# bf16 copies stored over six steps, the second step's tokens loaded later, half of the high angle tables built by GpSimd, the first statistics moved behind the recurrence

## The chip, the cores and the metric

The kernel runs on all eight cores of one Trainium2 chip. Each core takes one of the eight sequences, computes it alone and exchanges nothing with the others. The time is that of the slowest core, in microseconds of the device. Five engines have instruction streams of their own: PE (TensorE, matrix products), DVE (VectorE), ACT (ScalarE), POOL (GpSimd) and SP (SyncE, which here only issues transfers). Transfers run on 16 DMA engines per core, fed by a queue of SP and a queue of POOL.

## The reference

One sequence has 8192 tokens of 1024 numbers. What is computed, cut to the core:

```python
xn = layernorm(x)                                   # over the 1024 features
# recurrence, complex, one state per p (1024 of them)
Lambda = exp(-exp(nu_log) + 1j*exp(theta_log))
Bu = einsum('ph,blh->blp', (B_re + 1j*B_im)*exp(gamma_log)[:, None], xn)
xs[t] = Lambda * xs[t-1] + Bu[t]
s  = real(einsum('hp,blp->blh', C_re + 1j*C_im, xs)) + D*xn
# feed-forward, 1024 -> 4096 -> 1024
g  = silu(relu(xn @ W1 + b1) @ W2 + b2)
out = x + s*g
```

The inputs and weights are float32; the kernel multiplies in bfloat16 and adds up in float32.

## The kernel before

The 8192 tokens go through in 16 steps of 512 (`NSTEP`). In every step all weights pass through SBUF once: they are laid out as 24 chunks (`NCH`) of 128 x 4096 numbers, in the order c0 to c23 of the list `ORDER`: B0, W1_0, B1, W1_1, B2, W1_2, B3, W1_3, W1_4 to W1_7, W2_0 to W2_3, C_0 and C_1, W2_4 to W2_7, C_2 and C_3. A chunk of B, W1 or W2 is used by 32 matmuls of 512 columns. The two C chunks of a half are used together, by 64 matmuls (`cx`), and no earlier than both have landed. The chunks share five slots (`RING = 5`, n % 5, where n = 24 k + c counts chunks over the steps): chunk n may be loaded when the matmuls of chunk n-5 are done (`consumed`).

A chunk gets into its slot in one of two ways. A **cast** (line 257) reads 2 MB of float32 from HBM and writes 1 MB of bfloat16 into the slot; POOL issues it. A **load** (line 215) reads the 1 MB of bfloat16 that the kernel has stored in its HBM tensor `wb`; SP issues it. The **store** of that copy (`keep`, line 200) is issued by SP from the slot, once the cast has landed; until it has landed the slot can't be refilled. `KEEP_STEP[c]` is the step in which chunk c is stored: up to that step it is cast, after it loaded. SP's queue also carries the tokens x of the next step (2 MB, line 231; for step 1 line 221) and the results, two halves of 1 MB per step (lines 224, 227). SP goes through n = 0, 1, 2, ... in order: at place n come the load of n if it is one, the store of chunk n-4 if it is due, then tokens and results. Whatever it waits for holds back all that stands behind it. POOL goes through the casts in order in the same way.

In a step, PE computes Bu for state groups m = 0 to 7 (128 states each, two per B chunk, line 322) between the first W1 chunks (line 333), then W2's first half (line 345), C's first half (line 360), W2's second half with the transposes of the next step's tokens between (line 288), and C's second half. ACT copies Bu out of PSUM into one of four buffers `vv` (line 433, buffer m % 4, which needs DVE's first two products on group m-4 to be done, `v_u`) and the W1 results into `h1` (line 439). Its order is fixed: vv0, vv1, four of h, vv2, vv3, four of h, ..., so that a late `vv` holds back the h behind it, and with them PSUM banks 4 to 7, which PE's W1 groups take in turn. For group m, DVE turns Bu back by the angle of each token with tables of cosines and sines (`cS`, `sS`, 512 columns for each of the eight groups), runs the real recurrence (line 636) and turns the result forward again (`state`, lines 626 to 654). C needs all eight groups (`v_xs`).

The tables are built in step 0 by DVE, by doubling: level lv fills columns 2^lv to 2^(lv+1) from the ones below with six instructions (`double`, lines 574 to 581). Levels 0 to 5 are done for all groups at once (`tables_low`), levels 6 to 8 for groups 0 to 3 before group 0 and for groups 4 to 7 before group 4 (`tables_high`). The statistics of the next step's layer norm (`ln_stats`, lines 506 to 513) come before group 7.

Of the kernel before, what the change touches and what calls it, by code (L numbers as in the profile page):

```python
# [10 lines left out]
ALU = mybir.AluOpType  # L11
# [4 lines left out]
N = 512  # L16
NSTEP = T // N
CH = H // 128
# [16 lines left out]
PLACE = {c: i for i, c in enumerate(ORDER)}  # L35
RING = 5

KEEP_STEP = [(0, 2, 1, 2)[c % 4] for c in range(NCH)]


def is_cast(n):
# [16 lines left out]
def build_program():  # L58
# [15 lines left out]
    def sem(name):  # L74
        return es.enter_context(nc.semaphore(name))
# [66 lines left out]
    v_out = sem("v_out")  # L142

    p_id = sem("p_id")

    nu, th, gam, b1 = par[:, 0:8], par[:, 8:16], par[:, 16:24], par[:, 24:56]
    r_tab = ab[:, 0:8]
# [44 lines left out]
    def sync_program(eng):  # L192
# [17 lines left out]
        for n in range(NCH * NSTEP):  # L210
            k, c = n // NCH, n % NCH
            if not is_cast(n):
                slot_free(n)
                eng.wait_ge(*kept(first_kept(n)))
                eng.dma_start(ring[n % RING][:, :],
                              bass.AP(wb_d.ap().tensor, c * 128 * 4096,
                                      [[4096, 128], [1, 4096]])).then_inc(d_w[n % RING], 16)
            if n >= RING - 1 and is_kept(n - RING + 1):
                keep(n - RING + 1)
            if n == 8:  # L220
                eng.dma_start(xt[1][:, :], x_rows(1)).then_inc(d_x[1], 16)
            if c == NCH - 1:
                eng.wait_ge(v_out, 8 * k + 4)
                eng.dma_start(out_rows(k, 0), xt_half(k, 0)).then_inc(d_out[0], 16)
            if c == 5 and k >= 1:
                eng.wait_ge(v_out, 8 * k)
                eng.dma_start(out_rows(k - 1, 1), xt_half(k - 1, 1)).then_inc(d_out[1], 16)
            if c == 8 and 1 <= k < NSTEP - 1:
                for h in range(2):
                    eng.wait_ge(d_out[h], 16 * k)  # L230
                eng.dma_start(xt[(k + 1) % 2][:, :], x_rows(k + 1)
                              ).then_inc(d_x[(k + 1) % 2], 16)
# [11 lines left out]
    def gpsimd_program(eng):  # L244
        eng.memset(dx[:, 0:128], 1.0).then_inc(p_id, 1)
        eng.wait_ge(p_id, 1)
        eng.affine_select(dx[:, 128:256], dx[:, 0:128], [[1, 128]], ALU.is_equal, 0.0,
                          base=0, channel_multiplier=-1).then_inc(p_id, 1)
        eng.wait_ge(d_x0[1], 16)
        for n in range(3 * NCH):  # L250
            if not is_cast(n):
                continue
            if n >= RING:
                eng.wait_ge(*consumed(n - RING))
                if is_kept(n - RING):
# [2 lines left out]
                          bass.AP(w_d.ap().tensor, (n % NCH) * 128 * 4096,  # L258
                                  [[4096, 128], [1, 4096]])
                          ).then_inc(d_cast[n % RING], 16)  # L260
            if n == 6:
                for dst, src in ((d_rep, dv_d), (b2_rep, b2_d)):
                    eng.dma_start(dst[:, :], bass.AP(src.ap().tensor, 0, [[0, 128], [1, H]])
                                  ).then_inc(d_rows, 16)
# [222 lines left out]
    def vector_program(eng):  # L487
# [93 lines left out]
            t = mark(eng.tensor_tensor(seg(sS, n), seg(sS, n), tb_, ALU.add))  # L581
            eng.wait_ge(*t)

        def tables_low():

            mark(eng.memset(view(cS, 0, [[CH * N, 128], [N, CH]]), 1.0))
            t = mark(eng.memset(view(sS, 0, [[CH * N, 128], [N, CH]]), 0.0))
# [13 lines left out]
            eng.wait_ge(*t)  # L601
            for lv in range(6):
                double(lv, 0, CH)
            mark(eng.tensor_copy(c512, lad[:, 144:152]))
            mark(eng.tensor_scalar(view(ab, 32, [[64, 128], [2, 8]]), lad[:, 152:160], -1.0, None,
                                   ALU.mult))
            mark(eng.tensor_copy(view(ab, 33, [[64, 128], [2, 8]]), lad[:, 152:160]))

        def tables_high(first):
            for lv in range(6, 9):  # L610
                double(lv, first, 4)

        P1, P2 = pq[:, 0:2 * N], pq[:, 2 * N:4 * N]

# [78 lines left out]
        first_finish(2)  # L693
        angles()
        first_finish(3)
        tables_low()
        for k in range(NSTEP):
            turn[0] += CI
            for m in range(CH):
                if k == 0 and m % 4 == 0:  # L700
                    tables_high(m)
                if m == CH - 1 and k + 1 < NSTEP:
                    ln_stats(k + 1)
                state(k, m)
            if k + 1 < NSTEP:
                ln_finish(k + 1)
            if k == 0:
# [55 lines left out]
```

## Time and profile before

| | us |
|---|---|
| median of 3 runs (lowest, highest) | 2754.15 (2751.19, 3036.26) |
| profiled execution, its own time | 2755.06 |
| span of its slowest core, core 4 | 2753.9 |
| span of its fastest core, core 1 | 2727.4 |
| PE busy, share of the span | 2683.8, 97% |
| DVE busy | 1906.7, 69% |
| POOL busy | 30.6, 1% |

The span runs from the first to the last instruction of a core; the device's own time of the profiled execution is 1.2 us more. Busy time of PE counts overlapping matmuls whole, so the starts in its timeline say more than its sum. All rows below are of core 4 where nothing else is said. A row of the timeline stands for a run of like instructions; what stands in brackets is the idle time before it and what ended that.

### The profile page before, as it was taken

How to read it: one execution, taken by the hardware profiler on the slowest of the kernel's cores; microseconds unless marked ns; L12 is line 12 of the kernel's file. 1: busy time of each engine (PE TensorE's matmuls, PEld its weight loads, DVE VectorE, ACT ScalarE, POOL GpSimd, SP SyncE). 2: the span in 40 equal slices, each digit the busy share in tenths (PEclk: the TensorE clock that was granted, in tenths of full speed). 3: DMA queues.
4: the chain of work that ended last, by engine and by line, in shares of the span. 5: the costliest groups of instructions: out<-in, count | busy, mean ns of one | idle time of the engine just before them, and what ended most of it. 6: DMA issues, size and time to landing. Idle time of an engine off the chain costs nothing.

```text
span 2753.9 us, 35106 instructions; the slowest of 8 cores (2727.4 to 2753.9 us)
## 1 busy us (share of the span) xinstructions
PE 2683.8 (97%) x12545; PEld 1235.0 (45%) x12800; DVE 1906.7 (69%) x2684; ACT 765.5 (28%) x1018; POOL 30.6 (1%) x62
## 2 busy tenths in 40 slices
PE   6889998999999999999999999999999999999999
PEld 3344443444444444444444444444444444444444
DVE  7949659287593965849577594875939759395674
ACT  4222323223232322313223132231322323132220
POOL 1000000000000000000000000000000000000000
PEclk9999999999999999999999999999999999999998
DMA  9999988874544545445454454545545355464542
GB/s 189 190 186 211 211 199 226 237 256 143 184 183 168 199 145 187 182 146 213 163 204 154 160 201 161 198 153 182 185 164 197 136 191 184 153 214 151 180 153 99
DMA packets 84793, 498.28 MB, mean 181 GB/s; under 512 B 7568, under 2 KB 7568, under 8 KB 32400
## 3 DMA queue, kind: packets, MB, share of 16 engines
q1 hardware_dynamic: 76560, 438.36, 45.1%
q0 software_dynamic: 8064, 57.68, 13.0%
q8 instruction: 105, 1.72, 0.3%
q14 instruction: 64, 0.52, 0.1%
HBM read 493.91 MB, written 58.72 MB: 201 GB/s over the span
## 4 chain that ended last, share of the span: by engine, by line
PE 89%; DMA 10%; issue 1%; DVE 1%; SPq 0%; DVEq 0%; POOLq 0%
PE PS L345 31%; PE PS L333 27%; PE PS L360 16%; PE PS L322 13%; DMA wb<-ring 4%; DMA ring<-w 4%; PE PS L288 1%; DMA out<-xt 1%; DMA ring<-wb 0%; DMA xt<-x 0%; PE PS L301 0%; DVE dx L679 0%; DVE xt L682 0%; DVE dx L676 0%; DVE dx L672 0%
## 5 line engine op out<-in xcount | busy, mean ns | idle before, releaser
L333 PE MATMUL PS<-xT,ring 128*128 128x512 bf16 x4001 | 893.5, 381 | 29.6 <-DMA ring<-w 16.3
L345 PE MATMUL PS<-ring,h 128*128 128x512 bf16 x4017 | 892.1, 380 | 4.2
L333 PEld LDWEIGHTS PS<-xT,ring 128*128 128x128 bf16 x4096 | 402.1, 98 | 513.2 <-issue 34.4
L345 PEld LDWEIGHTS PS<-ring,h 128*128 128x128 bf16 x4096 | 398.7, 98 | 470.7 <-issue 6.9
L659 DVE TENSOR_TENSOR gg<-PS,b_rep 128x512 f32<-128x512 f32 x128 | 88.3, 692 | 613.6 <-PE PS L345 613.6
L439 ACT ACTIVATE h<-PS,par_s 128x512 bf16<-128x512 f32 x512 | 352.5, 689 | 519.5 <-PE PS L333 518.4
L322 PE MATMUL PS<-xT,ring 128*128 128x512 bf16 x1999 | 447.3, 379 | 2.0 <-DMA ring<-w 0.2
L636 DVE TENSOR_TENSOR_SCAN yy<-ab,carry,pq 128x512 f32<-128x512 f32 x256 | 314.2, 1269 | 0.0
L322 PEld LDWEIGHTS PS<-xT,ring 128*128 128x128 bf16 x2032 | 198.7, 98 | 240.2 <-issue 0.7
L433 ACT ACTIVATE vv<-PS,ab 128x1024 bf16<-128x1024 f32 x128 | 142.8, 1116 | 537.5 <-PE PS L322 513.5
L360 PE MATMUL PS<-ring,xsr 128*128 128x512 bf16 x1006 | 243.8, 382 | 7.8 <-DMA ring<-w 6.7
L360 PE MATMUL PS<-ring,xsi 128*128 128x512 bf16 x994 | 242.8, 382 | 1.6
L427 ACT ACTIVATE xT<-PS 128x512 bf16<-128x512 f32 x128 | 69.7, 596 | 472.8 <-PE PS L288 472.7
L627 DVE TENSOR_TENSOR pq<-vv,cS 128x1024 f32<-128x1024 bf16 x128 | 156.8, 1225 | 28.6 <-DVE xsi L652 16.6
L360 PEld LDWEIGHTS PS<-ring,xsr 128*128 128x128 bf16 x1024 | 100.7, 98 | 129.9 <-issue 13.8
L643 DVE TENSOR_TENSOR pq<-yy,cS 128x1024 f32<-128x1024 f32 x128 | 156.1, 1219 | 0.2 <-issue 0.2
L647 DVE TENSOR_TENSOR pq<-yy,sS 128x1024 f32<-128x1024 f32 x128 | 156.2, 1220 | 0.0
L360 PEld LDWEIGHTS PS<-ring,xsi 128*128 128x128 bf16 x1024 | 100.8, 98 | 123.0 <-issue 6.8
L628 DVE TENSOR_TENSOR pq<-vv,sS 128x1024 f32<-128x1024 bf16 x128 | 155.9, 1218 | 0.0
L676 DVE TENSOR_TENSOR dx<-dx,PS 128x512 f32<-128x512 f32 x128 | 88.1, 689 | 72.3 <-PE PS L360 55.9
L446 ACT ACTIVATE gg<-gg 128x512 f32<-128x512 f32 x128 | 78.9, 629 | 170.9 <-DVE gg L659 170.7
L679 DVE TENSOR_TENSOR dx<-dx,gg 128x512 f32<-128x512 f32 x128 | 88.6, 693 | 23.2 <-DVE dx L676 23.2
(72 smaller groups left out, 1023.8 us busy)
## 6 DMA issues: line engine op xcount, KB each, us to landing
ring<-wb SPq DMA_DIRECT2D x330, 1024.0 KB, 4.9
ring<-w POOLq DMA_DIRECT2D x54, 1024.0 KB, 17.6
out<-xt SPq DMA_DIRECT2D x31, 1024.0 KB, 8.8
xt<-x SPq DMA_DIRECT2D x15, 2048.0 KB, 10.1
wb<-ring SPq DMA_DIRECT2D x24, 1024.0 KB, 14.5
xt<-x SPq DMA_DIRECT2D x4, 512.0 KB, 7.2
out<-xt SPq DMA_DIRECT2D x4, 256.0 KB, 2.0
d_rep<-Dv POOLq DMA_DIRECT2D x1, 512.0 KB, 30.4
```

The source lines that it names most:

```text
L322: inst = eng.matmul(bk(2 * (m % 2) + comp), w[:, o:o + 128], xT[:, kc * N:(kc + 1) * N], start=(kc == 0), stop=(kc == CH - 1))
L333: inst = eng.matmul(bk(b), w[:, o:o + 128], xT[:, kc * N:(kc + 1) * N], start=(kc == 0), stop=(kc == CH - 1))
L345: inst = eng.matmul(bk(tb), h1[:, o:o + 128], w[:, kl * 512:(kl + 1) * 512], start=(q == 0 and kl == 0), stop=(q == 3 and kl == 7), skip_g ...
L360: inst = eng.matmul(bk(b), xs[:, o:o + 128], w[comp][:, pc * 512:(pc + 1) * 512], start=(comp == 0 and pc == 0), stop=(comp == 1 and pc == ...
L433: eng.activation(vv[m % 4][:, :], bk(2 * (m % 2), 2), AF.Identity, scale=gam_t[:, m:m + 1]).then_inc(a_vv, 1)
L439: eng.activation(h1[:, mi * N:(mi + 1) * N], bk(b), AF.Relu, bias=b1[:, mi:mi + 1]).then_inc(a_h1, 1)
L627: mark(eng.tensor_tensor(p1, u3, cc, ALU.mult))
L628: t = mark(eng.tensor_tensor(p2, us, ss, ALU.mult), v_u)
L636: y = mark(eng.tensor_tensor_scan(yy[:, j * N:(j + 1) * N], rb, wb, carry[:, 2 * m + j:2 * m + j + 1], ALU.mult, ALU.add))
L643: q = mark(eng.tensor_tensor(p1, y3, cc, ALU.mult))
L647: q = mark(eng.tensor_tensor(p2, ys, ss, ALU.mult))
L679: t = mark(eng.tensor_tensor(dx[:, :], dx[:, :], gg[:, tb * 512:(tb + 1) * 512], ALU.mult))
```

## The change

Four edits. (1) `KEEP_STEP` becomes a list by chunk with values 0 to 5, where it was 0, 2, 1, 2 in turn: 2 chunks are stored in step 0, 1 in step 1, 2 in step 2, 4 in step 3, 9 in step 4 and 6 in step 5. A chunk is cast until it is stored, so there are 107 casts, where there were 54, and POOL's loop goes over six steps. (2) The tokens of step 1 are requested when chunk 8 has been used, not before. (3) Levels 6 to 8 of the tables of groups 4 to 7 are built by POOL, in six parts of three instructions, one part behind each of the casts n = 6 to 11; DVE waits for them before group 4. DVE builds the other half where it did. The copies of D and b2 to all partitions are issued behind cast 14, not 6. (4) The statistics of step 1 come behind group 7, not before it, and so do not stand between groups 6 and 7 in step 0; in the other steps they stay.

```diff
-KEEP_STEP = [(0, 2, 1, 2)[c % 4] for c in range(NCH)]
+KEEP_STEP = [4, 5, 4, 3, 4, 5, 4, 4, 2, 5, 4, 3, 1, 4, 5, 0, 3, 4, 5, 2, 4, 0, 3, 5]
+LAST_KEEP = max(KEEP_STEP)
...
             if n == 8:
+                eng.wait_ge(*consumed(n))
                 eng.dma_start(xt[1][:, :], x_rows(1)).then_inc(d_x[1], 16)
...
+        def high_part(j):
+
+            lv, half = 6 + j // 2, j % 2
+            n = 1 << lv
+
+            def seg(tab, at):
+                return bass.AP(tab, 4 * N + at, [[CH * N, 128], [N, 4], [1, n]])
+
+            def each(off):
+                return bass.AP(lad, lv * 16 + off + 4, [[160, 128], [1, 4], [0, n]])
+
+            tmp = bass.AP(gg, half * 4 * 256, [[TB * 512, 128], [n, 4], [1, n]])
+            if j == 0:
+                eng.wait_ge(v_tab, 4)
+            elif half == 0:
+                eng.wait_ge(p_tab, 3 * j)
+            if half == 0:
+                eng.tensor_tensor(tmp, seg(sS, 0), each(8), ALU.mult).then_inc(p_tab, 1)
+                eng.tensor_tensor(seg(cS, n), seg(cS, 0), each(0), ALU.mult).then_inc(p_tab, 1)
+                eng.wait_ge(p_tab, 3 * j + 2)
+                eng.tensor_tensor(seg(cS, n), seg(cS, n), tmp, ALU.subtract).then_inc(p_tab, 1)
...
         eng.wait_ge(d_x0[1], 16)
-        for n in range(3 * NCH):
+        for n in range((LAST_KEEP + 1) * NCH):
             if not is_cast(n):
                 continue
...
-            if n == 6:
+            if 6 <= n <= 11:
+                high_part(n - 6)
+            if n == 14:
                 for dst, src in ((d_rep, dv_d), (b2_rep, b2_d)):
...
-        def tables_low():
+        def tables():
...
-            mark(eng.tensor_copy(c512, lad[:, 144:152]))
+            mark(eng.tensor_copy(c512, lad[:, 144:152]), v_tab)
...
-        def tables_high(first):
             for lv in range(6, 9):
-                double(lv, first, 4)
+                double(lv, 0, 4)
...
             for m in range(CH):
-                if k == 0 and m % 4 == 0:
-                    tables_high(m)
-                if m == CH - 1 and k + 1 < NSTEP:
+                if k == 0 and m == 4:
+                    eng.wait_ge(p_tab, 18)
+                if m == CH - 1 and 1 <= k < NSTEP - 1:
                     ln_stats(k + 1)
                 state(k, m)
+            if k == 0:
+                ln_stats(1)
```

POOL's order in step 0, from its first cast on, before (`ring` is a slot, `w` the float32 weights):

```order
L257 DMA ring<-w 128x4096 x7
L263 DMA d_rep<-Dv 128x1024
L263 DMA b_rep<-b 128x1024
L257 DMA ring<-w 128x4096 x47
```

and in the changed kernel, from the fourth part on (`gg` holds the temporary product, `lad` the factors of each level):

```order
L288 DMA ring<-w 128x4096
L275 TENSOR_TENSOR gg<-cS,lad 128x512
L276 TENSOR_TENSOR sS<-sS,lad 128x4x128
L278 TENSOR_TENSOR sS<-sS,gg 128x4x128
L288 DMA ring<-w 128x4096
L270 TENSOR_TENSOR gg<-sS,lad 128x1024
L271 TENSOR_TENSOR cS<-cS,lad 128x4x256
L273 TENSOR_TENSOR cS<-cS,gg 128x4x256
L288 DMA ring<-w 128x4096
L275 TENSOR_TENSOR gg<-cS,lad 128x1024
L276 TENSOR_TENSOR sS<-sS,lad 128x4x256
L278 TENSOR_TENSOR sS<-sS,gg 128x4x256
L288 DMA ring<-w 128x4096 x3
```

Three products or sums on 256, 512 or 1024 numbers per partition now stand between two casts on POOL's stream.

SP's order over steps 0 and 1 before, from the tokens of step 0 on:

```order
L205 DMA xt<-x 128x1024 x3
L200 DMA wb<-ring 128x4096 x2
L221 DMA xt<-x 128x4x1024
L200 DMA wb<-ring 128x4096 x3
L224 DMA out<-xt 128x4x512
L215 DMA ring<-wb 128x4096
L200 DMA wb<-ring 128x4096
```

and in the changed kernel:

```order
L207 DMA xt<-x 128x1024 x3
L224 DMA xt<-x 128x4x1024
L202 DMA wb<-ring 128x4096
L227 DMA out<-xt 128x4x512
L202 DMA wb<-ring 128x4096
L230 DMA out<-xt 128x4x512
L234 DMA xt<-x 128x4x1024
L217 DMA ring<-wb 128x4096
```

Of the six stores of step 0 two are left, and none stands before the tokens of step 1.

## Rows read from the trace of the kernel before

**Rows 1.** The page: busy time, share and instructions of PE.
```profile
PE 2683.8 (97%) x12545; PEld 1235.0 (45%) x12800; DVE 1906.7 (69%) x2684; ACT 765.5 (28%) x1018; POOL 30.6 (1%) x62
```

**Rows 2.** Span and granted clock of two cores.
```profile
core 1: 2727.4 us, clock 0.996
...
core 4: 2753.9 us, clock 0.991
```

**Rows 3.** Timeline of PE: start, length, instructions, [idle before <-what ended it].
```profile
83.97 37.24 PE L333 MATMUL PS<-xT,ring 128*128 128x512 bf16 x157 [11.05 <-DMA ring<-w]
...
155.58 2.29 PE L360 MATMUL PS<-ring,xsr 128*128 128x512 bf16 x5 [6.74 <-DMA ring<-w]
...
215.20 7.07 PE L322 MATMUL PS<-xT,ring 128*128 128x512 bf16 x31
...
266.48 29.26 PE L333 MATMUL PS<-xT,ring 128*128 128x512 bf16 x125 [2.77 <-DMA ring<-w]
298.26 7.07 PE L333 MATMUL PS<-xT,ring 128*128 128x512 bf16 x31 [2.52 <-DMA ring<-w]
...
389.83 7.07 PE L322 MATMUL PS<-xT,ring 128*128 128x512 bf16 x31
...
467.20 1.87 PE L333 MATMUL PS<-xT,ring 128*128 128x512 bf16 x4 [8.14 <-DMA ring<-wb]
...
567.76 7.07 PE L322 MATMUL PS<-xT,ring 128*128 128x512 bf16 x31
581.58 7.07 PE L322 MATMUL PS<-xT,ring 128*128 128x512 bf16 x31
...
735.31 7.07 PE L322 MATMUL PS<-xT,ring 128*128 128x512 bf16 x31
```

**Rows 4.** DMA queues from 85 to 155 us: packets, MB, share of 16 engines.
```profile
q0 software_dynamic: 1410, 10.24, 93.0%
q1 hardware_dynamic: 339, 2.43, 8.6%
```

**Rows 5.** The same queue and stretch on core 1.
```profile
q0 software_dynamic: 1437, 10.46, 90.4%
```

**Rows 6.** The page: SP's queue over the whole span.
```profile
q1 hardware_dynamic: 76560, 438.36, 45.1%
```

**Rows 7.** Chain of waits from 215 to 300 us: start, length, what.
```profile
248.87 36.63 DMA wb<-ring
...
286.02 12.00 DMA ring<-w
```

**Rows 8.** Timeline of DVE in step 0.
```profile
48.98 1.23 DVE L627 TENSOR_TENSOR pq<-vv,cS 128x1024 f32<-128x1024 bf16 x1 [0.17 <-DVE sS L581]
...
81.24 1.22 DVE L628 TENSOR_TENSOR pq<-vv,sS 128x1024 f32<-128x1024 bf16 x1
...
90.39 0.43 DVE L574 TENSOR_TENSOR pq<-sS,lad 128x256 f32<-128x256 f32 x1
...
103.48 1.23 DVE L627 TENSOR_TENSOR pq<-vv,cS 128x1024 f32<-128x1024 bf16 x1 [0.17 <-DVE sS L581]
...
134.60 4.85 DVE L506 BATCH_NORM_STATS2 st<-xt 128x6 f32<-128x512 f32 x8 [0.17 <-DVE xsi L652]
...
140.19 1.23 DVE L627 TENSOR_TENSOR pq<-vv,cS 128x1024 f32<-128x1024 bf16 x1
...
149.70 0.69 DVE L652 SCALAR_TENSOR_TENSOR xsi<-pq 128x512 bf16<-128x512 f32 x1
```

**Rows 9.** Busy time (instructions) of PE, PEld, DVE, ACT, POOL; clock, DMA share, GB/s.
```profile
35.00:90.00 55.00, 43.51 (x187) 18.97 (x190) 52.62 (x71) 14.30 (x18) 4.78 (x9) 0.88 0.98 197
```

**Rows 10.** Timeline of ACT in step 0.
```profile
82.55 1.11 ACT L433 ACTIVATE vv<-PS,ab 128x1024 bf16<-128x1024 f32 x1 [9.25 <-DVE pq L628]
87.64 0.69 ACT L439 ACTIVATE h<-PS,par_s 128x512 bf16<-128x512 f32 x1 [3.98 <-PE PS L333]
```

**Rows 11.** Timeline of POOL in step 0.
```profile
1.40 0.29 POOL L247 TENSOR_SCALAR_AFFINE_SELECT dx<-dx 128x128 f32<-128x128 f32 x1
...
38.54 0.53 POOL L257 DMA_DIRECT2D ring<-w  x1 [2.61 <-PE PS L333]
...
73.47 0.53 POOL L257 DMA_DIRECT2D ring<-w  x1 [6.77 <-PE PS L322]
```

More of the change, by code:

```diff
@@ L144, in build_program @@
     p_id = sem("p_id")
+    p_tab = sem("p_tab")
     nu, th, gam, b1 = par[:, 0:8], par[:, 8:16], par[:, 16:24], par[:, 24:56]
@@ L248, in gpsimd_program @@
                           base=0, channel_multiplier=-1).then_inc(p_id, 1)
+        def high_part(j):
[15 more added lines that the diff above has]
+                eng.tensor_tensor(seg(cS, n), seg(cS, n), tmp, ALU.subtract).then_inc(p_tab, 1)
+            else:
+                eng.tensor_tensor(tmp, seg(cS, 0), each(8), ALU.mult).then_inc(p_tab, 1)
+                eng.tensor_tensor(seg(sS, n), seg(sS, 0), each(0), ALU.mult).then_inc(p_tab, 1)
+                eng.wait_ge(p_tab, 3 * j + 2)
+                eng.tensor_tensor(seg(sS, n), seg(sS, n), tmp, ALU.add).then_inc(p_tab, 1)
         eng.wait_ge(d_x0[1], 16)
-        for n in range(3 * NCH):
+        for n in range((LAST_KEEP + 1) * NCH):
             if not is_cast(n):
@@ L695, in vector_program @@
         first_finish(3)
-        tables_low()
+        tables()
         for k in range(NSTEP):
```

## The prediction, made before the changed kernel ran

> **What bounds the kernel now.** I read the page first: PE is busy for 97% of the span [rows 1]. The timeline of PE tells what that hides. From step 3 on a step takes 735.31 - 567.76 = 167.55 us without an idle gap, and a chunk 6.91 us, half of the distance between the two B rows at 567.76 and 581.58 [rows 3]. 24 chunks make 165.8; the other 1.75 are the transposes. So 13 of 16 steps are at PE's own pace, and no edit touches them. Time can only come or go before 568 us. Core 4 loses it at five places [rows 3]: 11.05 us idle before W1_3, 6.74 before C in step 0; 2.77 and 2.52 in step 1, which takes 389.83 - 215.20 = 174.63, that is 7.1 over; 8.14 in step 2, which takes 177.93, 10.4 over. The overs are more than the idle because PE comes back at half clock: from 83.97 to C, less the idle, lie 64.87 us for nine chunks that need 62.2, so a long gap costs 2.7 more. Every one of these gaps ends with a transfer into the ring.
>
> The DMA queues say why. Between 85 and 155 us both queues together fill more than the whole of the 16 engines [rows 4]. A cast costs 0.93 x 70 us / (10.24 MB / 1.049) = **6.67 us** of all 16; 1 MB on SP's queue costs 0.451 x 2753.9 / (438.36 / 1.049) = **2.97 us** [rows 2, 4, 6]. A step's transfers, counted so (each has 4 MB of tokens and results): step 1 has 18 casts, 6 loads, 6 stores: 167.6 us; step 2 has 12, 12, 12: 163.2. Both are just under PE's 167.55 and still lost 7.1 and 10.4. The chain of waits shows how: a store issued right behind the tokens' load took 36.63 us, POOL could refill its slot only then, and 12 us later PE got its chunk [rows 7].
>
> **The change, part by part.**
>
> *Stores over six steps.* Step 0 loses four stores and gains nothing: 24 casts and 8 MB, 183.9 us. Steps 1 to 4 become (casts, loads, stores) 22, 2, 1: 167.5; 21, 3, 2: 166.8; 19, 5, 4: 165.3; 15, 9, 9: 165.4. Step 5 (6, 18, 6) has 123.2 and is free. So two steps at 97 to 100% become four. Bounds for what such a step loses: 0, since none is over 167.55, and 10.4, the worst seen. Less store traffic speaks for the low end, and in steps 1 to 3 no store stands directly behind the tokens' load; in step 4 those of c6 and c7 do. Against it: five slots are a lead of at most four chunks, the tokens and one half of the results (9 us) fall together in each step's first half, where eight chunks of PE (55.3) meet eight casts (53.4) in steps 1 to 3, and each pair of C chunks wants the second 6.9 us early. I take the nearer row, 7.1, for each of the four: **28.4 us**, in place of 17.5.
>
> A page bears on the price: the Trainium skill, HBM Reference, § on the domain's bandwidth, says that the two cores of a pair share about 716 GB/s, some 358 each when both stream. By it a cast's 2.1 MB would be an estimated 5.9 us, and step 1 would need about 150 and lose nothing. The row, taken with all eight cores casting, has 6.67, and decides.
>
> *Later tokens.* The 2 MB (5.9 us) leave the stretch before W1_3, and so do two stores (5.9) and the D and b2 copies (3.0), while that chunk was 11.05 late. W1_3 then starts on time, near 72.9. What is late next is ACT: its vv for group 7 waited for DVE's second product on group 3 (81.24 + 1.22) and ended at 83.66 [rows 8, 10]; the first h behind it ends near 84.4 and frees the bank for W1_4. So W1_4 starts at 84.4 + L, where L is what DVE is late by then. Tokens asked for when W1_4 is done, near 111, land by 150 even if they take as long as that store did; wanted behind group 7.
>
> *High tables on POOL.* DVE loses 103.48 - 90.39 = 13.1 us between groups 3 and 4 [rows 8]; it is in nobody's way, because W1_4 depends on groups 0 to 3, and C on all eight. POOL gets 18 instructions with 3 x 2 x (256 + 512 + 1024) = 10,752 numbers per partition. The trace has no POOL product of two tensors. Low: DVE's rate, 1.22 us per 1024: 12.8 us. High: POOL's one row of arithmetic, 0.29 us for 128: 24.4 us [rows 8, 11]. The parts run between 38.5 and some 85 us, behind casts whose times PE sets [rows 11]; with at most 7 us for the longest they delay the next cast by about one cast's issue, and end before DVE wants them. What matters is L: whether POOL's reads of the same SBUF tables hold DVE, which is busy 52.62 of 55 us there [rows 9], so that nothing held is given back. Bounds for L: 0 (independent), 24.4 (each holds the other). Casts issued by POOL do not stretch a group of DVE, 10.4 us each, but they read no table. I take L = **20**, near the upper end: both engines work on two SBUF operands at once, and POOL's own row is the nearer price.
>
> The Trainium skill, SBUF — State Buffer, § on the shared port pair, speaks against this edit: DVE with two SBUF inputs and a GpSimd instruction that reads SBUF exclude each other for a whole instruction. Nothing in this trace tests it; by it L is all of POOL's time, without it the first rival below holds.
>
> With L = 20, W1_4 starts at 104.4; eight chunks and the half clock (55.3 + 2.7) give C at **162.4**. Group 7 ends at 150.4 - 13.1 - 5.6 + 20 = 151.7, not in the way, and the second C chunk, which landed by 155.3, has four stores less ahead of it and one more: 146.4. From C to the end of the step are eight chunks and the transposes, 57.0: 219.4, against 215.20: **+4.2**.
>
> *Statistics behind group 7.* Saves 140.19 - 134.60 = 5.6 us before C [rows 8]; C is 10 us later than group 7 already, so nothing. They end near 157, before W2's results.
>
> Sum against the profiled execution: 2755.06 + 4.2 + 28.4 - 17.5 = **2770 us**. Its time is 1 us above the median of the runs.
>
> **Rivals.** *POOL costs DVE nothing* (L = 0). For it: POOL's casts leave DVE's groups alone. Against: no row has both on tables. C then starts at 146.4, when its chunk lands, the step ends near 206 with half clock, -9.2: 2755.1 - 9.2 + 10.9 = **2757**.
>
> *The four steps lose nothing* (the queue's few stores are worth more than its casts). For: core 1, with 0.904 x 70 / (10.46 / 1.049) = 6.35 us per cast, has the shortest span [rows 2, 5]. Against: the slowest core counts, at 6.67. With L = 20 **2742**, with L = 0 **2728**, the only case that is plainly faster.
>
> *Casts get dearer when six steps stream them*: slower than before by over 2%. Place: steps 1 to 4 on every core, all of them over PE's pace. Each 0.1 us per cast is 7.7 us over their 77 casts. At 7.3 us they need 181.4, 180.0, 177.3 and 174.8, in all 43.3 over, which gives 2813; 7.25 is the point from which it decides. Against it: step 0 had this traffic, on eight cores, at 6.67.
>
> **How the numbers follow.** Chances: the forecast (L from 12 to 24, a loss of 5 to 10 per step) 0.46; L near 0 with the losses 0.24; L with no losses 0.14; neither 0.10; dearer casts 0.04; the rest spread, 0.02. The likeliest case gives 2770. Upper bound of its terms: L = 24.4 (+8.6) and 10.4 per step (+41.6 - 17.5): 2788. The range takes in 2742 and 2757 and leaves out 2728 and 2813: **2738 to 2788**. Nearly all cases lie within 2%, which is about what a measurement of this kernel can tell from no change: faster by over 2% (below 2700) 0.01, within 0.95, slower 0.04.
>
> **What the profile after would show.** W1_3 on time near 73 and a gap before W1_4, ended through ACT by DVE, 5 us long if L = 0 and 25 if L = 20. DVE's products of 1024 numbers longer than 1.22 us, or gaps between them, while POOL has a part: L in its sum. POOL's 18 instructions, 13 to 24 us in all. C in step 0 at 146 or 162. PE's gaps in steps 1 to 4, ended by casts, 28 in sum with the clock; step 4 with one before W1_7 or W2_0 behind the stores of c6 and c7. Steps from 5 on at 167.55. I am wrong if a gap grows in step 5 or later, if W1_3 is still late, or if casts leave 6.3 to 6.7 us.

## The result

| | us |
|---|---|
| before, beside it (median of its runs) | 2754.15 |
| after (median; lowest and highest of 5 runs) | 2766.18 (2765.5, 2766.25) |
| ratio after / before, with its 95% interval | 1.0053 [1.0035, 1.0071] |
| profiled execution, its own time | 2766.18 |
| span of its slowest core, core 3 | 2765.1 |
| span of its fastest core, core 7 | 2751.5 |

The change costs 0.5%, some 12 to 15 us; the interval allows 10 to 20. Executions in which some cores show a lower granted clock are left out of every range of times below, and of the ratios where the difference is marked, and rows come from cores and stretches that show none of it. All rows are of the slowest such core where nothing else is said. The line numbers have moved: B is line 355, W1 366, W2 378, C 393 of the changed kernel; ACT's vv 466 and h 472; DVE's first two products of a group 659 and 660.

The page has this in place of [rows 1]:

```profile
PE 2694.4 (97%) x12800; PEld 1233.6 (45%) x12800; DVE 1914.6 (69%) x2666; ACT 763.3 (28%) x1018; POOL 87.1 (3%) x133
```

PE's share is the same 97%, and again that row hides everything that happened. POOL has gone from 30.6 to 87.1 us. What answers to [rows 3] is the timeline of PE:

```profile
77.08 5.68 PE L355 MATMUL PS<-xT,ring 128*128 128x512 bf16 x16 [8.64 <-ACT vv L466]
82.60 7.07 PE L366 MATMUL PS<-xT,ring 128*128 128x512 bf16 x32
104.34 29.88 PE L366 MATMUL PS<-xT,ring 128*128 128x512 bf16 x128 [14.68 <-ACT h L472]
163.77 1.89 PE L393 MATMUL PS<-ring,xsr 128*128 128x512 bf16 x8 [1.92 <-DMA ring<-w]
220.81 7.07 PE L355 MATMUL PS<-xT,ring 128*128 128x512 bf16 x32
...
393.76 7.07 PE L355 MATMUL PS<-xT,ring 128*128 128x512 bf16 x32
...
561.58 7.07 PE L355 MATMUL PS<-xT,ring 128*128 128x512 bf16 x32
...
622.27 30.32 PE L366 MATMUL PS<-xT,ring 128*128 128x512 bf16 x128 [5.28 <-DMA ring<-wb]
737.09 7.07 PE L355 MATMUL PS<-xT,ring 128*128 128x512 bf16 x32
...
818.08 8.75 PE L366 MATMUL PS<-xT,ring 128*128 128x512 bf16 x32 [3.62 <-DMA ring<-wb]
831.24 29.47 PE L378 MATMUL PS<-ring,h 128*128 128x512 bf16 x128 [4.41 <-DMA ring<-wb]
917.59 7.07 PE L355 MATMUL PS<-xT,ring 128*128 128x512 bf16 x32
```

The starts of B0 (220.81, 393.76, 561.58, 737.09, 917.59) give the steps 172.95, 167.82, 175.51 and 180.50: 5.4, 0.3, 8.0 and 12.95 over PE's pace of 167.55, together **26.6**. The next step is at that pace and stays there.

Step 0 changed the name of its wait. The gap before W1_4 ends with ACT, and behind ACT stands DVE, which is late because of this (POOL first, then DVE in the same stretch):

```profile
66.14 1.91 POOL L270 TENSOR_TENSOR gg<-sS,lad 128x1024 f32<-128x1024 f32 x1
68.00 1.89 POOL L271 TENSOR_TENSOR cS<-cS,lad 128x1024 f32<-128x1024 f32 x1
70.03 2.61 POOL L273 TENSOR_TENSOR cS<-cS,gg 128x1024 f32<-128x1024 f32 x1
```
```profile
65.96 4.49 DVE L683 TENSOR_TENSOR xsr<-pq 128x512 bf16<-128x512 f32 x1
70.37 2.82 DVE L684 SCALAR_TENSOR_TENSOR xsi<-pq 128x512 bf16<-128x512 f32 x1
...
82.27 0.69 DVE L683 TENSOR_TENSOR xsr<-pq 128x512 bf16<-128x512 f32 x1
```

Read the two together; `xsr` and `xsi` are the two results of a group that C reads. POOL's products at 66.14 and 68.00 end at 69.89. DVE's instruction for `xsr`, which takes 0.69 us when POOL is quiet (82.27), is recorded from 65.96 and ends at 70.45: it ends 0.56 us, most of its own length, after POOL's pair. The next one ends at 73.19, 0.55 us after POOL's third at 72.64. So in these rows the two engines do not share, they take turns, and the waiting is inside DVE's recorded length: busy time hides it. Between 66 and 93 us no DVE row names POOL as what it waited for.

### The profile page after: what moved, and what is told of

Read it like the earlier page. It is cut to its first block, busy times and chain, and to the rows that moved or that the text cites. A ratio compares the mean times of both kernels' runs of the same rounds, so it can differ in the third digit from the quotient of the medians.

```text
span 2765.1 us, 35310 instructions; the slowest of 8 cores (2751.5 to 2765.1 us)
## 1 busy us (share of the span) xinstructions
PE 2694.4 (97%) x12800; PEld 1233.6 (45%) x12800; DVE 1914.6 (69%) x2666; ACT 763.3 (28%) x1018; POOL 87.1 (3%) x133
## 4 chain that ended last, share of the span: by engine, by line
PE 85%; DMA 10%; DVE 3%; issue 1%; ACT 0%; DVEq 0%; SPq 0%; POOL 0%; POOLq 0%; ACTq 0%
PE PS L378 30%; PE PS L366 27%; PE PS L393 15%; PE PS L355 13%; DMA wb<-ring 5%; DMA ring<-w 4%; PE PS L321 1%; DMA ring<-wb 1%; DVE pq L659 0%; DVE pq L660 0%; DMA xt<-x 0%; DVE yy L668 0%; DVE xsr L683 0%; DVE pq L608 0%; DVE xsi L684 0%
## 5 line engine op out<-in xcount | busy, mean ns | idle before, releaser
L366 PE MATMUL PS<-xT,ring 128*128 128x512 bf16 x4096 | 901.8, 381 | 26.1 <-ACT h L472 14.7
## 6 DMA issues: line engine op xcount, KB each, us to landing
xt<-x SPq DMA_DIRECT2D x15, 2048.0 KB, 11.3
```

What stands on the lines that cost most here:

```text
L366: inst = eng.matmul(bk(b), w[:, o:o + 128], xT[:, kc * N:(kc + 1) * N], start=(kc == 0), stop=(kc == CH - 1))
```

## The experiments

All are compared with the kernel before, run beside them. "Over" is always a step's length less 167.55. The theory of the prediction was that POOL's reading instructions hold DVE in step 0 (L = 20), and that the casts take most of what the transfers of steps 1 to 4 have to spare. The rivals to be told apart were a step 0 without L and steps without losses. The eight cores run the same program and still differ by up to 17 us in what they lose, so a row of one core is not enough; a table behind the runs has all of them.

**1. The high tables by DVE again**, everything else as changed:

```diff
-            if 6 <= n <= 11:
-                high_part(n - 6)
...
-                    eng.wait_ge(p_tab, 18)
+                    for lv in range(6, 9):
+                        double(lv, 4, 4)
```

> The changed kernel, except that DVE again builds levels 6 to 8 of groups 4 to 7, before group 4; POOL computes nothing in step 0. Theory (POOL's products hold DVE, L = 20 us, and this alone makes W1_4 late): DVE's instructions between 38 and 92 us are back at 1.22 and 0.69 us, the gap before W1_4 shrinks to about 5 us, C of step 0 starts at about 146 in place of 164, and the time is 2766 - 13 = 2753 us, give or take 4. Rival (DVE is late because casts, not products, hold it): the gap before W1_4 stays above 13 us and the time near 2766. Second rival (the lead that PE's long gap gave the queue is worth as much as the gap): steps 1 to 4 lose over 35 us in place of 27, and the time stays at 2762 or more.

Measured: 2752.9 to 2760, median 2757.1, ratio 1.0006 [0.9994, 1.0019]: as expected, at the upper edge. PE on the slowest core, 7, of an execution that took 2759.95:

```profile
83.55 29.74 PE L364 MATMUL PS<-xT,ring 128*128 128x512 bf16 x128 [5.11 <-ACT h L470]
...
207.49 7.07 PE L353 MATMUL PS<-xT,ring 128*128 128x512 bf16 x32
```

W1_4 starts 20.8 us earlier (83.55 against 104.34) and step 0 ends 13.3 us earlier. But the next four steps start at 207.49, 378.90, 547.60, 726.08 and 911.28: 3.9, 1.1, 10.9 and 17.65 over, 33.6 in place of 26.6. On the slowest core of this execution half of what step 0 gives is taken again. That is not the rule: the ratios, 1.0053 and 1.0006, differ by 13 us, which is all that step 0 gives, and over all cores the four steps lose 4 us more on average. This is the rival "POOL costs DVE nothing" made real, and at its price of 2757.

**2. The high tables on POOL alone**, put into the kernel before (edit 3 with its wait, no other):

```diff
+            if 6 <= n <= 11:
+                high_part(n - 6)
...
+                if k == 0 and m == 4:
+                    eng.wait_ge(p_tab, 18)
```

> The kernel before with edit 3 alone: POOL builds the high tables of groups 4 to 7 behind casts 6 to 11; the store list, the tokens and the statistics are as before. Theory: L = 20 again, whatever the list is: W1_4 starts near 104 in place of 93.6, C of step 0 near 162, step 0 ends 4 us later than before; with a fuller ring behind the long gap steps 1 and 2 lose a little less than their 17.5 us: 2755 to 2760. Rival (the loss needs the changed list's casts): 2754 with W1_4 at 94.

Measured: 2754.2 to 2758.4, ratio 1.0004 [0.9992, 1.0016]. The copies of D and b2 stay behind cast 6 here. On core 1:

```profile
104.81 30.29 PE L365 MATMUL PS<-xT,ring 128*128 128x512 bf16 x128 [13.09 <-ACT h L471]
...
219.60 7.07 PE L354 MATMUL PS<-xT,ring 128*128 128x512 bf16 x32
```

The same start of W1_4 (104.8) and end of step 0 (219.6) as in the full change, so L is edit 3's and no other's. It costs 4.4 us against [rows 3] there, 3.9 on the average of all cores, and the interval of the whole time has no change in it. Steps 1 and 2 lose 10.0 and 10.1, where a little less than 17.5 in sum was expected.

**3. The stores over six steps alone**, in the kernel before:

```diff
-KEEP_STEP = [(0, 2, 1, 2)[c % 4] for c in range(NCH)]
+KEEP_STEP = [4, 5, 4, 3, 4, 5, 4, 4, 2, 5, 4, 3, 1, 4, 5, 0, 3, 4, 5, 2, 4, 0, 3, 5]
```

> The kernel before with edit 1 alone, the new list of stores. Theory: step 0 gains, since no store stands before W1_3: that chunk is on time or nearly, W1_4 waits about 4 us for DVE's group 3, C of step 0 waits for DVE's group 7 at 150.4 in place of its chunk at 155.3, and step 0 ends about 5 us earlier than before; steps 1 to 4 lose 27 us as in the changed kernel, in place of 17.5 in steps 1 and 2: 2754 - 5 + 9 = 2758, give or take 5. Rival (spreading the stores is worth what it was made for): 2740 or less.

Measured: ratio 1.0023 [1.0012, 1.0034], runs of 2758.6 to 2764: at the upper edge of what was expected. Core 5:

```profile
149.36 3.57 PE L361 MATMUL PS<-ring,xsr 128*128 128x512 bf16 x8 [11.03 <-DVE xsi L653]
```

Step 0 ends at 209.02; its C waits for DVE, not for a chunk. The steps after lose 6.3, 0, 10.2 and 17.25: 33.8, as in run 1. The stores alone win 6 us in step 0 and lose 16 behind it. The losses are there without edits 2, 3 and 4.

**4. Later tokens and the moved statistics alone** (edits 2 and 4), in the kernel before:

```diff
             if n == 8:
+                eng.wait_ge(*consumed(n))
...
-                if m == CH - 1 and k + 1 < NSTEP:
+                if m == CH - 1 and 1 <= k < NSTEP - 1:
...
+            if k == 0:
+                ln_stats(1)
```

> The kernel before with edits 2 and 4 alone: the tokens of step 1 are requested when chunk 8 is used, the statistics of step 1 come behind group 7. Theory (both only move work within step 0): W1_3 is late by about 5 us in place of 11, but the tokens then stand before C's chunks, which land at about 155 as before; DVE is done with group 7 at 145 and waits for nobody: 2754, give or take 3, with up to 3 us lost again before the transposes, because the statistics hold back the combination of the results. Rival (each edit gives what it takes off its place, 6 and 5.6 us): 2743.

Measured: 2750.5 to 2753.6, ratio 1.0007 [0.9995, 1.002], as expected. Core 1:

```profile
76.23 36.06 PE L334 MATMUL PS<-xT,ring 128*128 128x512 bf16 x160 [3.05 <-DMA ring<-w]
128.56 23.38 PE L346 MATMUL PS<-ring,h 128*128 128x512 bf16 x96 [9.36 <-DMA ring<-w]
```

The wait before W1_3 falls to 3.05 us and one of 9.36 appears before W2_1, where the tokens now are. Step 0 ends at 215.16, against 215.20 in [rows 3]; over all cores it ends at 206.4 to 217.0, before at 208.8 to 217.2. The traffic was moved, not removed.

**5 and 6. What on POOL holds DVE?** Two kernels like run 1 (DVE builds all tables), in which POOL also carries 18 instructions that nobody uses, at the same six places, on a buffer of its own that DVE never touches. In the first they are products of two SBUF operands, in the second they only write, over twice as many numbers. This idle work, with one more write of that buffer at the start and DVE's wait for the work before group 4, is all that is added.

```diff
+            for i in range(3):
+                eng.tensor_tensor(t, t, t, ALU.mult).then_inc(p_tab, 1)
```
```diff
+            for i in range(3):
+                eng.memset(t, 1.0).then_inc(p_tab, 1)
```

> As tables_dve (DVE builds all tables; 2757 us), but POOL computes beside it what nobody uses: behind casts 6 to 11 three products each on private data in gg, with 256, 512 and 1024 numbers per partition as in the changed kernel. Theory (POOL and DVE exclude each other as engines, whatever the addresses): DVE's instructions stretch as in the changed kernel, W1_4 starts near 104 again in place of 83.5, C of step 0 near 163 to 165 (group 7 is 13 us later than in the changed kernel), and the time is 2768 to 2775. Rival (they clash because both read the same tables cS and sS and the factors in lad): DVE stays at 1.22 us, W1_4 at 84, 2757 us.

> As dummy_products, but POOL's instructions only write: 18 memsets of 512, 1024 and 2048 numbers per partition, which read nothing. Theory (it is POOL's reading beside DVE's two operands that holds DVE): DVE stays at 1.22 us, W1_4 at 84, and the time is tables_dve's 2757, give or take 4. Rival (any POOL instruction on SBUF holds DVE for as long as it runs): DVE is late by most of POOL's busy time, W1_4 after 92, 2765 or more.

Measured: products 2769 to 2770, ratio 1.0065 [1.005, 1.008]; writes 2751.8 to 2756.4, ratio 0.9995 [0.9977, 1.0013]. PE, POOL and DVE of core 1 with the products:

```profile
102.40 29.57 PE L351 MATMUL PS<-xT,ring 128*128 128x512 bf16 x128 [14.68 <-ACT h L457]
```
```profile
66.26 7.05 POOL L263 TENSOR_TENSOR gg<-gg 128x1024 f32<-128x1024 f32 x3
```
```profile
66.24 2.48 DVE L669 SCALAR_TENSOR_TENSOR xsi<-pq 128x512 bf16<-128x512 f32 x1
68.89 2.66 DVE L644 TENSOR_TENSOR pq<-vv,cS 128x1024 f32<-128x1024 bf16 x1 [0.17 <-DVE xsi L669]
```

And with the writes, core 1 again, PE, POOL and DVE:

```profile
83.08 7.29 PE L350 MATMUL PS<-xT,ring 128*128 128x512 bf16 x23 [5.31 <-ACT h L456]
```
```profile
65.02 5.67 POOL L262 MEMSET gg<- 128x2048 f32 x3
```
```profile
67.56 0.69 DVE L668 SCALAR_TENSOR_TENSOR xsi<-pq 128x512 bf16<-128x512 f32 x1
68.42 1.23 DVE L643 TENSOR_TENSOR pq<-vv,cS 128x1024 f32<-128x1024 bf16 x1 [0.17 <-DVE xsi L668]
```

The windows from 38 to 93 us on core 1 say the same in one row each (us, then busy time and count of PE, PEld, DVE, ACT, POOL; clock, DMA share, GB/s). Run 1, run 5, run 6:

```profile
38.00:93.00 55.00, 50.22 (x224) 22.16 (x222) 52.75 (x68) 17.02 (x22) 3.52 (x7) 0.94 1.02 167
```
```profile
38.00:93.00 55.00, 42.54 (x190) 18.58 (x188) 53.65 (x42) 10.88 (x14) 32.61 (x25) 0.93 0.92 156
```
```profile
38.00:93.00 55.00, 49.69 (x221) 21.89 (x219) 52.68 (x68) 16.80 (x22) 22.52 (x24) 0.94 0.97 163
```

DVE is almost equally busy in all three, 52.7 to 53.7 us, but gets through 68 instructions, 42 and 68. That count is where a stretched engine shows; its busy time does not. W1_4 is as late with products on a private buffer as with the tables, so it is not the shared tables that couple the engines. POOL's writes, 22 us of busy time, hold nobody. They also stand between two casts on POOL's stream for almost as long as the products (5.67 us in the row above, 7.05 with the products), so it is not later casts that make DVE late. A POOL instruction that reads one operand only was not tried.

**7. The stores of c6 and c7 in step 5, not 4**, on run 1:

```diff
-KEEP_STEP = [4, 5, 4, 3, 4, 5, 4, 4, 2, 5, ...]
+KEEP_STEP = [4, 5, 4, 3, 4, 5, 5, 5, 2, 5, ...]
```

> As tables_dve, with c6 and c7 stored in step 5 in place of step 4; two more casts. Theory (step 4 loses its 16 to 18 us because these two stores stand behind the tokens in SP's queue and their slots are wanted first by c11 and c12): step 4 loses under 7 us, step 5 gains no gap over 2 us, the gap of 6 to 8 us before c8 in step 3 stays (it is c3's store behind the results), and the time is 2757 - 11 = 2746, give or take 4. Rival (the number of bytes decides): step 4 loses as much and step 5 some more, 2757 or above.

Measured: ratio 1.0024 [1.0003, 1.0045], 2752 to 2756. A miss by 6 to 10 us, and by the ratio no faster than run 1. Core 0's steps from 1 on lose 2.7, 0.6, 6.8, **3.1** and **8.5**; over all eight cores step 4 loses 2.8 to 7.0, where run 1 loses 13.3 to 17.7, and step 5 loses 6.8 to 10.7. Step 4 gave what was expected; step 5, which loses nothing in the kernels above, now has this:

```profile
994.25 16.53 PE L376 MATMUL PS<-ring,h 128*128 128x512 bf16 x63 [5.79 <-DMA ring<-w]
```

Its chain of waits goes back through four stores in a row, three of which are shown. The first of them was issued 0.48 us behind the tokens' load, and SP had held both back until the results had landed:

```profile
895.86 31.77 DMA out<-xt
...
927.71 0.38 SPq L234
...
928.19 17.29 DMA wb<-ring
...
946.01 8.44 DMA wb<-ring
...
965.32 12.52 DMA wb<-ring
978.36 15.64 DMA ring<-w
```

So the two stores are what step 4 could not bear, and a step 5 with 8 stores can't either, though its transfers, 8 casts, 16 loads, 8 stores and 4 MB, sum to 136.5 us at the prediction's prices. The sum over a step is not the test.

**8. Another list**, on run 1: the stores are 2, 1, 2, 4, 6 and 9 from step 0 to 5, and are so placed that few follow each other; 110 casts in place of 107.

```diff
-KEEP_STEP = [4, 5, 4, 3, 4, 5, 4, 4, 2, 5, 4, 3, 1, 4, 5, 0, 3, 4, 5, 2, 4, 0, 3, 5]
+KEEP_STEP = [4, 5, 3, 4, 0, 5, 3, 5, 4, 2, 2, 5, 1, 4, 5, 5, 3, 0, 3, 5, 4, 5, 5, 4]
```

> As tables_dve, with another list of stores: 4 5 3 4 0 5 3 5 4 2 2 5 1 4 5 5 3 0 3 5 4 5 5 4, 110 casts in place of 107, and 2, 1, 2, 4, 6, 9 stores in steps 0 to 5. No store that is followed soon by a reload of its slot stands behind a long transfer of tokens or results. Theory (the losses of steps 1 to 4 come from the places of the stores in SP's queue, not from the number of casts): steps 1 to 5 lose under 5 us in all, and the time is 2753 - 24 = 2729 us, give or take 5. Rival (DMA engines are simply full in four steps, 97 to 100% of PE's pace): as many casts lose as much, 2750 or more.

Measured: 2736.5 to 2739.9, ratio 0.9938 [0.9918, 0.9959]. Faster than before although it has more casts, and slower than expected by some 10 us, outside the 5 that were allowed. Core 4's steps from 1 on lose 0, 0, 3.5, 4.55 and 5.6; the other seven cores lose 0.2 to 5.4 in all. In steps 1 to 3 this list has as many casts, loads and stores as run 1's, only other chunks, so there the places alone count, and on all cores the three steps lose 0 to 3.7 in place of 4.4 to 16. In step 4 it also has fewer stores, 6 for 9, and the run doesn't tell the two apart.

**9 and 10. Tokens and results issued by ACT**, so that SP's queue holds nothing but loads and stores; once on run 1, once on the kernel before. The edit is the same:

```diff
 SP:
-            if c == 5 and k >= 1:
-                eng.wait_ge(v_out, 8 * k)
-                eng.dma_start(out_rows(k - 1, 1), xt_half(k - 1, 1)).then_inc(d_out[1], 16)
...
 ACT:
+                if i == 0 and k >= 1:
+                    eng.wait_ge(v_out, 8 * k)
+                    eng.dma_start(out_rows(k - 1, 1), xt_half(k - 1, 1)).then_inc(d_out[1], 16)
...
+                if mi == 16 and 1 <= k < NSTEP - 1:
+                    ...
+                    eng.dma_start(xt[(k + 1) % 2][:, :], x_rows(k + 1)
+                                   ).then_inc(d_x[(k + 1) % 2], 16)
```

> As tables_dve (2757 us, and 32 to 34 us lost in steps 1 to 4), but from step 1 on the tokens, and in all steps but the last the results, are issued by ACT, so that they have a queue of their own and SP carries only stores and loads of the ring. The bytes are the same. Theory (a store lands late because it stands behind 2 MB of tokens or 1 MB of results in SP's queue): stores in steps 3 and 4 land in under 20 us in place of 30 to 33, the gap before c8 in step 3 falls from 6 to 8 us to under 2, step 4 loses under 7 us in place of 16 to 18, and the time is 2757 - 20 = 2737 us, give or take 6. Rival (the engines are simply full, whoever is first): the same bytes take the same time, only other transfers are late, 2752 or more.

> The kernel before with tokens and results on ACT's queue in the same way. Theory: steps 1 and 2, which lose 7.1 and 10.4 us on core 4 by stores that stand behind the tokens, lose under 6 together; step 0 is as before: 2753 - 12 = 2741, give or take 5. Rival: unchanged, 2753.

Measured: 2745.5 to 2749, ratio 0.998 [0.9941, 1.0019], on run 1; 2752.8 to 2757.6, ratio 1.0003 [0.9974, 1.0031], on the kernel before. Both missed, the second whole. On the first, core 0 loses 4.3, 0, 1.5 and 11.8, and core 7 nothing in step 3. Step 3 loses 3.7 to 10.9 by core in run 1 and 0 to 1.55 here: that loss was the store's place in SP's queue. Step 4's is not, or not alone; it is 13.3 to 17.7 there and still 10.5 to 13.8 here. Core 0:

```profile
790.28 16.07 PE L356 MATMUL PS<-xT,ring 128*128 128x512 bf16 x64 [5.29 <-DMA ring<-w]
810.26 27.79 PE L368 MATMUL PS<-ring,h 128*128 128x512 bf16 x128 [3.91 <-DMA ring<-wb]
```
```profile
767.54 27.22 DMA wb<-ring
```

A store there takes 27.22 us with neither tokens nor results on its queue. On the kernel before, step 1 loses 9.4 to 10.9 by core, where it lost 0.9 to 7.6, and step 2 loses 0 to 9.5, where it lost 0 to 10.4. On core 4, the fastest here, step 2 is clean; on core 2, the slowest, it loses 6.9. So the edit did not free step 2, and step 1 is worse on every core. PE and DVE of core 4, then PE of core 2:

```profile
325.95 3.57 PE L352 MATMUL PS<-ring,xsr 128*128 128x512 bf16 x8 [6.80 <-DVE xsi L655]
```
```profile
309.70 4.85 DVE L509 BATCH_NORM_STATS2 st<-xt 128x6 f32<-128x512 f32 x8 [23.40 <-DMA xt<-x]
```
```profile
336.01 2.29 PE L352 MATMUL PS<-ring,xsr 128*128 128x512 bf16 x5 [8.86 <-DVE xsi L655]
```

On core 4 the tokens, asked for at 265.85, landed after 43.76 us; DVE idled 23.40 us for them in front of group 7, and C waited for DVE. In step 1 the stores' wait had turned into the tokens'.

**11 and 12. List and queue together**, and then with the tokens asked for earlier, behind the results of W1_2 in place of the first of W1_4:

```diff
+                if i == 2 and 1 <= k < NSTEP - 1:
...
-                if mi == 16 and 1 <= k < NSTEP - 1:
```

> other_list (0.9938 of before, about 2737 us) with tokens and results on ACT's queue. Its steps 3 to 5 still lost 3 to 14 us by core. Theory: they lose under 5, and the time is 2731 to 2735; what is left is step 0, which ends at 206 to 207. Rival (that list leaves nothing behind the tokens, so the queue no longer matters): 2737.

> act_other_list with the tokens asked for by ACT behind W1_2's results, some 15 to 25 us earlier in each step, in place of behind W1_4's. Theory (in act_other_list and act_before they landed 44 us after they were asked for, so that DVE's statistics before group 7, and C behind them, waited): the gaps of 1.4 to 1.6 us before C in steps 1 and 3 (6.8 in act_before) are gone, no new wait comes, 2730 to 2733. Rival (tokens and ring transfers then collide as they did on SP's queue): gaps before c8 to c12 return, 2737 or more; or ACT waits for the results' landing and holds back h, which would show as PE gaps ended by ACT in each W1_4.

Measured: 2732.5 to 2734.4, ratio 0.9929 [0.9898, 0.996], as expected; and 2728.0 to 2728.8, ratio **0.9907 [0.9888, 0.9926]**, just below the 2730 that was the lower end. The intervals of runs 8, 11 and 12 overlap, so that what the queue adds to the list is told by the cores' steps and not by the ratios. In run 11 one core still loses 9.6 us behind step 0, where under 5 was expected. Core 0 of the last:

```profile
144.01 1.89 PE L383 MATMUL PS<-ring,xsr 128*128 128x512 bf16 x7 [3.25 <-DVE xsi L685]
...
207.29 7.07 PE L345 MATMUL PS<-xT,ring 128*128 128x512 bf16 x31
```

Steps 1 to 5 lose 0, 0.35, 0, 1.6 and 0 (B0 starts at 374.84, 542.74, 710.28, 879.40 and 1046.94): 2 us, where the change lost 26.6. All eight cores lie between 2724.0 and 2726.9. What is left is step 0, and there DVE.

**All cores.** Where step 0 ends, and what steps 1 to 5 lose together, in us; lowest to highest core, mean in brackets.

| kernel | end of step 0 | lost in steps 1 to 5 |
|---|---|---|
| before | 208.8 to 217.2 (213.5) | 0.8 to 17.5 (9.1) |
| after | 216.2 to 221.0 (219.3) | 17.0 to 26.6 (21.3) |
| run 1 | 206.3 to 208.0 (207.1) | 19.7 to 33.6 (25.4) |
| run 2 | 216.1 to 219.6 (217.4) | 1.9 to 20.1 (12.5) |
| run 3 | 208.2 to 210.2 (209.2) | 17.9 to 33.7 (24.4) |
| run 4 | 206.4 to 217.0 (212.4) | 2.8 to 17.7 (11.3) |
| run 5, four cores | 223.8 to 225.7 (225.1) | 16.3 to 27.3 (21.4) |
| run 6 | 206.3 to 207.8 (207.1) | 16.8 to 27.1 (22.7) |
| run 7, six cores | 206.3 to 208.2 (207.4) | 15.7 to 28.6 (20.7) |
| run 8 | 206.6 to 208.7 (207.5) | 0.2 to 13.7 (3.8) |
| run 9, four cores | 207.1 to 209.7 (208.1) | 12.5 to 17.6 (14.9) |
| run 10 | 208.3 to 216.1 (212.3) | 9.4 to 19.8 (14.7) |
| run 11, six cores | 206.3 to 208.9 (207.8) | 0 to 9.6 (3.7) |
| run 12 | 206.2 to 208.8 (207.1) | 0 to 1.9 (0.5) |

## Why the prediction was right, step by step

**The sum.** It was 2755.06 + 4.2 + 28.4 - 17.5 = 2770, and the profiled execution has 2766.18. By the rows the terms are +5.6 (220.81 - 215.20), +26.6 and -17.5, which would give 2769.8. The other 3.6 lie at the very end: the last step of before, from 2578.32 to the end of the span at 2753.9, takes 175.6 us, that of after, from 2593.06 to 2765.1, takes 172.0. The windows of the last stretch, before and after:

```profile
2730.00:2750.00 20.00, 19.27 (x73) 7.83 (x72) 12.99 (x20) 1.26 (x2) 0.00 (x0) 0.81 0.10 39
```
```profile
2740.00:2760.00 20.00, 18.98 (x88) 8.39 (x86) 13.38 (x21) 2.52 (x4) 0.00 (x0) 1.00 0.07 28
```

Before, the granted clock of its last 20 us is 0.81, after it is 1.00. No edit is near it; the prediction took that tail over unseen. The other seven cores of before take 172.1 for that step, as all of after do. So the miss of 4 us is made of +1.4 in step 0, -1.8 in steps 1 to 4 and -3.6 in this tail, which is the largest of the three.

**L = 20.** Right: W1_4 starts at 104.34 (forecast 104.4), L = 104.34 - 84.4 = 19.9, and runs 2 and 5 have it in kernels without the rest of the change, run 1 without it. POOL's 18 instructions were to take 13 to 24 us and took 28.4, outside that range. But a record of theirs contains waiting too: six sets of three at the shortest lengths seen, 0.62 for 256 numbers, 1.04 for 512 and 1.9 for 1024, are 6 x 3.56 = 21.4 us. That is POOL's own work, and DVE was late by 19.9 of it. So each engine held the other, and L came near POOL's own work, for the reason that the prediction gave: both work on two SBUF operands at once. That its 20 hit 19.9 is in part luck: it was picked between 0 and 24.4, and the 24.4 came from an unlike instruction of POOL.

The Trainium skill, SBUF — State Buffer, in the part on the shared port pair, says that only a GpSimd instruction that reads SBUF excludes a DVE instruction with two SBUF inputs. Runs 5 and 6 agree: 18 products on a private buffer have W1_4 start at 101.0 to 102.9 by core, 18 writes at 83.1 to 83.9, and run 1 has 82.9 to 83.9.

**W1_3 on time near 73.** Half right. Its chunk no longer keeps PE waiting. But PE got to it at 82.60, since DVE's lateness stops PE first inside B3, 8.64 us at m = 7, and again before W1_4. The prediction had the whole of L in one gap of 25 us; it is two, 23.3 in all, against 11.05 before. The end is the same because both gaps come from the one chain.

**C at 162.4, end of step 0 at 219.4.** C_0 started at 163.77 after 1.92 us for its second chunk, which the prediction had as just in time. Group 7 ended at 151.8 (151.7). From C to the end 57.04 (57.0). So +5.6 and not +4.2; on the mean of all cores it is +5.8.

**Tokens and statistics of step 1.** No clear gain and no loss on the path, as said: run 4 ends step 0 at 206.4 to 217.0, before at 208.8 to 217.2. Where step 0 is short the place of the statistics counts: in run 3, with the statistics before group 7, C waits 11.03 us for DVE; in run 1, with edits 2 and 4 as well, C waits 3.50 and the first transposes 2.73, and step 0 ends 2.1 us earlier on average.

**Steps 1 to 4, 7.1 each.** The sum was right (26.6 for 28.4), the even split was not: 5.4, 0.3, 8.0, 12.95. A cast costs 0.82 x 280 / (37.52 / 1.049) = 6.42 us from 220 to 500 us, by the row of POOL's queue (packets, MB, share of 16 engines):

```profile
q0 software_dynamic: 5140, 37.52, 82.0%
```

which is below the 6.67 forecast and above 6.3. By HBM Reference of the Trainium skill a cast would be an estimated 5.9 us; neither stretch shows that. The prediction had the gaps end with casts; the largest, 5.28 in step 3 and 3.62 and 4.41 in step 4, end with loads. The chain of waits names two places:

```profile
573.46 33.28 DMA wb<-ring
...
606.85 15.19 DMA ring<-wb
...
773.86 30.50 DMA wb<-ring
...
804.89 19.51 DMA wb<-ring
...
824.51 6.49 DMA ring<-wb
```

In step 3 it is c3's store, directly behind a half of the results in SP's queue; the prediction looked only for stores behind tokens and found none in step 3. Run 9 takes results and tokens off that queue, and the loss of step 3 falls from 3.7 to 10.9 by core to 0 to 1.55. In step 4 it is c6 and c7, as predicted, and the gaps at 818 and 831 are before W1_7 and W2_0, as predicted. But tokens and results on the queue are not their cause alone: without them there the loss stays at 10.5 to 13.8. During the first eight chunks of step 4 the engines owe 7 casts, 1 load, 5 stores, the tokens and 1 MB of results: 7 x 6.67 + 9 x 2.97 = 73.4 us, where PE needs 55.3. With run 8's list it is 5 casts, 3 loads, 2 stores and the same 3 MB, 57.1, and the loss is 0 to 4.6 by core with SP's queue as it was and 0 to 1.6 with ACT's. The prediction's test, the sum over a whole step (165.4 of 167.55), missed this.

It is tempting to put the sum over the first eight chunks in its place, since five slots give at most four chunks of lead. The same sum for other steps doesn't bear that out:

| step | sum over c0 to c7 | lost, by core |
|---|---|---|
| after, 4 | 73.4 | 12.1 to 14.5 |
| run 7, 4 | 67.5 | 2.8 to 7.0 |
| after, 3 | 65.2 | 2.0 to 8.0 |
| run 8, 3 | 64.5 | 0 to 3.7 |
| after, 1 | 62.3 | 0 to 5.4 |
| after, 2 | 62.3 | 0 to 0.3 |
| before, 1 | 60.8 | 0.9 to 7.6 |
| before, 2 | 59.4 | 0 to 10.4 |
| run 7, 5 | 59.4 | 6.8 to 10.7 |
| run 8, 1 and 2 | 58.6 | 0 |
| run 8, 4 | 57.1 | 0 to 4.6 |
| run 8, 5 | 52.7 | 0 to 5.6 |

Only the heaviest step stands where the sum puts it. Below that, two steps at 59.4, both with four stores among these chunks, lose up to 10.4 and 10.7, while two at 62.3 with none lose up to 5.4 and 0.3. Number and place of the stores go together in most of these steps, so what each is worth in step 4 stays open.

**Are the terms independent?** The prediction added step 0 and the steps behind it as if they were. It also called step 1 of before "just under" PE's pace, where its own sum is 167.6 against 167.55. With this list of stores, the kernels with a long step 0 (after, run 5) lose 21.3 and 21.4 us on average behind it, those with a short one (runs 1, 3, 6) 25.4, 24.4 and 22.7. So there is a coupling of 1 to 4 us; the 7 us between the slowest cores of after and run 1 are more than is typical, and run 6, with a step 0 as short as run 1's, loses 27.1 at most. The difference between after and run 1 lies in steps 3 and 4 and not in step 1 (2.6 and 2.5 on average), so it is not a ring that was filled ahead during the long gap of step 0; its cause is open. That the rival with L = 0 was put at 2757 and run 1 came out at 2757.1 is partly luck: in the profiled execution, 2759.95, it had step 0 end at 206 (it was 207.5) and the four steps at 28.4 (33.6), with the tail's 3.6 us against that.

What stays open: why runs 9 and 10 lose 4.3 and 9.4 in step 1 is shown (late tokens), but not why step 4 of run 9 still loses 10.5 or more, nor by what rule the 16 engines divide themselves among three queues, so how late tokens come can only be measured. The version of run 12 was not tried with the statistics back before group 7 or with the stores' list tuned for ACT's queue.

## What to carry to other kernels

Before work is given to GpSimd, ask whether VectorE is busy on two SBUF operands at the same time; if so it cost VectorE nearly its whole length here (19.9 of 21.4 us), unless it only wrote. And don't trust the sum of a step's transfers, nor that of a shorter stretch: look at what stands directly behind each large transfer in its queue. In steps 1 to 3, with the same transfers, other places for the 1 MB stores took the loss from up to 16 us on a core (run 1) to 3.7 at most (run 8). Last, read every core: a fix that cleans a step on one core can leave it as it was on the slowest, as run 10 did.

## What the runs showed of the hardware

- In runs 5 and 6 the exclusion of VectorE and GpSimd goes by engine and by what the instruction reads, not by address: private operands make W1_4 nearly as late (101.0 to 102.9) as the shared tables (102.4 to 104.8), and a 0.69 us instruction is recorded as 4.49 us. GpSimd's writes (POOL busy 22.5 us) cost nothing (83.1 to 83.9).
- A product on GpSimd took 1.9 us for 1024 float32 numbers per partition, 1.04 for 512, against DVE's 1.22 for 1024.
- A 1 MB store took from 8.44 to 36.63 us from issue to landing in the rows above; the longest stood behind tokens or results in SP's queue (36.63, 33.28, 30.50), but one of 27.22 did not. 2 MB of tokens on ACT's queue took 43.76 us beside a stream of casts.
- The end of one core ran at a granted clock of 0.81 in the profiled execution of before, while the seven others took 172.1 us for the last step, and it took 175.6.
